# Second cross attention of a two-layer model: the delta scaled in the loop, both norms behind it in parts, and the mixtures fetched in order of use

## The reference, cut to what matters

```python
# fifth: second cross attention, 16 heads of 16, keys and values from audio tokens
delta = ctx @ Wo.T + bo
delta = clip(residual_scale, 0, 0.3) * delta
delta = (delta - mean(delta)) / sqrt(var(delta) + 1e-5) * ln_gamma + ln_beta
x = layernorm(x + delta)
# sixth: experts of the second layer
scores = softmax(x @ gate_weight.T)                 # 64 columns, the 6 largest are kept
flat = w_dense[:, inv_mapping]                      # 8 experts x 8 mixtures
soft = softmax(where(flat == 0, -1e9, flat)); scalar = flat.sum(-1)
# for each of the 8 experts f, with w = soft[f]:
xe = x + w @ muW.T
gate = silu(fused(xe, gW, qa, qb, scale, w)); up = fused(xe, ...)
out += scalar[f] * fused(gate * up, dW, dqa, dqb, ds, w)
y = out + shared(x)                                 # shared: silu(x @ G) * (x @ U) @ D
x = layernorm(x + y)
```

## Time and profile before

| what | value |
|---|---|
| median of three runs | 1113.26 us (1110.69 to 1115.44) |
| the profiled execution | 1109.19 us, its span 1107.4 us |
| mean granted TensorE clock | 0.931 |
| PE busy | 972.9 us, 88% of the span |
| DVE busy | 550.2 us, 50% |
| ACT busy | 362.3 us, 33% |
| POOL busy | 200.1 us, 18% |
| SP's DMA queue, share of 16 engines | 18.2% |

### The profile page before, as it was taken

The page is one execution under the profiler, slowest core; times in us unless marked ns, Lnnn a source line. Parts: engine busy times, 40 slices in busy tenths (PEclk is TensorE's granted clock), DMA queues, the critical chain, the costliest instruction groups (busy, mean ns, idle before and its releaser), DMA issues.

```text
span 1107.4 us, 18950 instructions
## 1 busy us (share of the span) xinstructions
PE 972.9 (88%) x7488; PEld 608.9 (55%) x7488; DVE 550.2 (50%) x1110; ACT 362.3 (33%) x724; POOL 200.1 (18%) x241
## 2 busy tenths in 40 slices
PE   7998879998899999983963899898498999999996
PEld 4664523333468899981452467758364444444443
DVE  2599788885431111015578576536762333233324
ACT  3444346666222233321366354143231000000002
POOL 5021000000012222210026841041000111111110
PEclk9999869999799999995987799998898999999998
DMA  6000000000745455523000202030015022221101
GB/s 235 2 2 1 1 1 2 2 2 1 276 141 180 149 186 188 170 86 115 1 1 1 76 2 97 1 136 3 1 47 119 13 87 87 81 77 66 37 1 38
DMA packets 27242, 75.15 MB, mean 68 GB/s; under 512 B 9860, under 2 KB 17292, under 8 KB 21780
## 3 DMA queue, kind: packets, MB, share of 16 engines
q1 hardware_dynamic: 24948, 67.91, 18.2%
q0 software_dynamic: 2208, 6.03, 1.8%
HBM read 67.48 MB, written 6.46 MB: 67 GB/s over the span
## 4 chain that ended last, share of the span: by engine, by line
PE 70%; DVE 21%; issue 3%; DMA 3%; ACT 3%; SPq 0%; POOL 0%; DVEq 0%; ACTq 0%; POOLq 0%
PE psum L1521 8%; PE psum L1096 8%; PE psum L1108 7%; DVE arena L2082 4%; PE psum L819 3%; PE psum L1525 3%; PE psum L1287 3%; PE psum L1551 3%; PE psum L1509 2%; PE psum L1555 2%; PE psum L1000 2%; DVE arena L2001 2%; DVE arena L2000 2%; PE psum L1546 2%; PE psum L1257 2%
## 5 line engine op out<-in xcount | busy, mean ns | idle before, releaser
L1944 ACT ACTIVATE arena<-psum 128x512 f32<-128x512 f32 (+1 forms) x32 | 19.0, 593 | 227.6 <-PE psum L1525 227.6
L1521 PE MATMUL psum<-arena 128*128 128x512 f32 (+1 forms) x192 | 90.6, 608 | 0.5 <-DVE arena L2530 0.5
L1762 ACT ACTIVATE arena<-psum,arena 128x128 f32<-128x128 f32 x184 | 52.4, 368 | 115.4 <-PE psum L1096 99.1
L2082 DVE TENSOR_REDUCE arena<-psum 128x2 f32<-128x512 f32 x128 | 82.6, 688 | 15.2 <-PE psum L946 13.1
L1096 PE MATMUL psum<-arena 128*128 128x128 f32 x736 | 86.7, 276 | 0.0
L1096 PEld LDWEIGHTS psum<-arena 128*128 128x128 f32 x736 | 84.0, 192 | 2.7 <-issue 2.7
L745 POOL TENSOR_TENSOR arena<-arena 128x512 f32<-128x512 f32 (+1 forms) x32 | 40.4, 1264 | 241.9 <-ACT arena L1944 241.9
L1108 PE MATMUL psum<-arena 128*128 x368 | 83.1, 379 | 0.0
L2229 DVE COPY arena<-psum 128x256 f32<-128x256 f32 x23 | 9.8, 425 | 135.6 <-PE psum L1081 85.2
L1739 ACT ACTIVATE arena<-psum 128x1024 f32<-128x1024 f32 x64 | 65.4, 1024 | 35.4 <-PE psum L968 32.5
L1108 PEld LDWEIGHTS psum<-arena 128*128 128x128 f32 x368 | 68.2, 190 | 8.4
(11 more groups left out here) (371 smaller groups left out, 1818.9 us busy)
## 6 DMA issues: line engine op xcount, KB each, us to landing
arena<-in_w SPq DMA_DIRECT2D x31, 1024.0 KB, 12.5
arena<-in_experts SPq DMA_DIRECT2D x8, 1248.0 KB, 5.9
arena<-mixed SPq DMA_DIRECT2D x16, 256.0 KB
arena<-mixed SPq DMA_DIRECT2D x8, 512.0 KB
arena<-in_ctx SPq DMA_DIRECT2D x2, 1024.0 KB, 7.4
arena<-returned SPq DMA_DIRECT2D x8, 256.0 KB, 5.0
arena<-in_w_xattn SPq DMA_DIRECT2D x1, 1538.5 KB, 9.9
arena<-in_w_ffn SPq DMA_DIRECT2D x1, 1152.0 KB, 5.2
```

What stands on the lines that cost most here:

```text
L1521: pe.matmul(out, e[w][:, k, :], xe6[:, half, k, :], start=(k == 0), stop=False)
L1762: last = act.activation(hidt[:, r % 2, ic * P:(ic + 1) * P], bank(n)[:, i * P:(i + 1) * P], ACT.Gelu, bias=b1_tile[:, r % 4, ic:ic + 1])
L2082: ax_max.by(dve.tensor_reduce(nmx[:, b % 2, :, h], bank(u % 2).rearrange("p (t s) -> p t s", t=2), AX.X, ALU.max, negate=True))
```

## The change

- `delta_stats` gets a fourth instruction, (delta - mean) * gamma, so the step of L2435 is done in the loop, tile by tile.
- Both norms are split. The norm of delta has two parts, tiles 0 to 4 (`FIRST5` = 5) and 5 to 7. The norm of x + delta has two parts, tiles 0 to 3 and 4 to 7. There are four additions of epsilon, four square roots on ACT (the first behind the last exponential of the attention loop, with its table load) and four inversions where there were two of each. The steps of the tiles alternate with `delta_stats(6)` and `delta_stats(7)`, and all go through `do`.
- `turn_x`, `copy_xt` and the logits are done by halves: four tiles transposed, their logits, four tiles transposed, their logits.
- `fetch_mix` issues `wm6` first, then `we6`, then `scale6`, each kind with a semaphore of its own (old semaphores are used again), and PE, DVE and POOL each wait for what they read only.
- PE's order at the start of the expert loop becomes `fuse_in(0)`, `shared_down(1, (0, 1))`, `ranks(0)`, `shared_down(1, (2, 3))`. `fuse_in(0)` waits for the fifth of the six shared products of DVE, since it writes the banks that these free.

The diff, without the new arguments `tiles`, `lo` and `hi` of `turn_x`, `copy_xt` and `ln_sqrt`, and without the waits of PE, DVE and POOL on the split semaphores (`near_in`, `mix_in`, `scale_in`):

```diff
@@ -476,7 +477,8 @@
         sh_h = again("sh_h", onx_ready, B)
         mixed_out = signal("mixed_out")
         mix_in = [signal(f"mix_in_{i}") for i in range(3)]
-        MIX_DMAS = 5
+        near_in = [Signal(loaded[n].sem, 32) for n in ("ident", "w_attn0", "w_xattn0")]
+        scale_in = [Signal(loaded[n].sem, base) for n, base in (("consts", 32), ("consts_late", 32), ("w_route0", 16))]
         scaled6 = signal("scaled6")
         tail_blank = signal("tail_blank")
         mid_dve = again("mid_dve", v_sb, 4)
@@ -593,14 +595,14 @@
             sp.dma_start(w_f1, a["w_ffn1"]).then_inc(loaded["w_ffn1"].sem, 16)
             def fetch_mix(f):
 
-                done, mixed = mix_in[f % BUFS], a["mixed"]
-                w = wide(mixed[f * KX:(f + 1) * KX, :], 1, RX)
+                mixed, buf = a["mixed"], f % BUFS
+                few = mixed[f * KX:(f + 1) * KX, :]
+                for k in range(KC):
+                    sp.dma_start(wm6[32 * k:32 * k + KX, buf, :], few).then_inc(near_in[buf].sem, 16)
                 for half in range(2):
-                    sp.dma_start(we6[64 * half:64 * half + 64, f % BUFS, :], w).then_inc(done.sem, 16)
-                sp.dma_start(scale6[:, f % BUFS, :], mixed[FX * KX + f:FX * KX + f + 1, :].to_broadcast([P, B * S]))\
-                  .then_inc(done.sem, 16)
-                for k in range(KC):
-                    sp.dma_start(wm6[32 * k:32 * k + KX, f % BUFS, :], mixed[f * KX:(f + 1) * KX, :]).then_inc(done.sem, 16)
+                    sp.dma_start(we6[64 * half:64 * half + 64, buf, :], wide(few, 1, RX)).then_inc(mix_in[buf].sem, 16)
+                sp.dma_start(scale6[:, buf, :], mixed[FX * KX + f:FX * KX + f + 1, :].to_broadcast([P, B * S]))\
+                  .then_inc(scale_in[buf].sem, 16)
 
             for f in range(FX):
                 if f == 2:
@@ -1555,13 +1557,14 @@
                     out6_ps.by(pe.matmul(tile_sum(4 * half + t), ha6[:, half, t * P:(t + 1) * P], e["dwx"], start=False,
                                          stop=(n >= STEPS - 2), skip_group_check=True))
 
-            turn_x(4)
             pe.wait_ge(loaded["w_ffn1"].sem, 16)
-            for j in range(NT):
-                pe.wait_ge(xt_sb.sem, 4 * NT + j + 1)
-                for k in range(KC):
-                    last = pe.matmul(bank(4)[:, j * E1:(j + 1) * E1], xt[:, k, j * P:(j + 1) * P],
-                                     f1["gate"][:, k, :], start=(k == 0), stop=(k == KC - 1))
+            for half in (range(0, 4), range(4, NT)):
+                turn_x(4, half)
+                for j in half:
+                    pe.wait_ge(xt_sb.sem, 4 * NT + j + 1)
+                    for k in range(KC):
+                        last = pe.matmul(bank(4)[:, j * E1:(j + 1) * E1], xt[:, k, j * P:(j + 1) * P],
+                                         f1["gate"][:, k, :], start=(k == 0), stop=(k == KC - 1))
             lg6_ps.by(last)
 
             def shared_down(n, tiles):
@@ -1597,13 +1600,15 @@
             for c4 in range(1, len(SHARED)):
                 gate_up(f1["shg"], f1["shu"], c4, 1)
             pe.wait_ge(wt6_sb.sem, wt6_sb.base + 2)
+            pe.wait_ge(sh_h.sem, sh_h.base + 2 * len(SHARED) - 1)
+            fuse_in(0)
             shared_down(1, (0, 1))
+            ranks(0)
+            shared_down(1, (2, 3))
             pe.wait_ge(tail_blank.sem, 1)
-            for step in range(-1, STEPS + 1):
+            for step in range(STEPS + 1):
                 if step + 1 < STEPS:
                     fuse_in(step + 1)
-                if step == -1:
-                    shared_down(1, (2, 3))
                 if 0 <= step < STEPS:
                     features(step)
                 if step + 1 < STEPS:
@@ -1902,13 +1907,16 @@
                 pt5_ready.by(act.activation(pt5[:, b % 2, :].rearrange("p (g n) -> p g n", g=2),
                                             s5[:, b // 2 % 2, :, b % 2 * D:(b % 2 + 1) * D], ACT.Exp,
                                             scale=attend5[:, b:b + 1], bias=off5[:, b:b + 1]))
+                if b == B - 1:
+                    ln_sqrt(4, 0, FIRST5)
                 if b % 2 == 1 and b >= 3:
                     copy_out5(b // 2 - 1)
             copy_out5(NT - 1)
-            ln_sqrt(4)
-            ln_sqrt(5)
-
-            copy_xt(4)
+            ln_sqrt(5, FIRST5, NT)
+            ln_sqrt(6, 0, 4)
+            copy_xt(4, range(0, 4))
+            ln_sqrt(7, 4, NT)
+            copy_xt(4, range(4, NT))
             act.wait_ge(p6_sub.sem, p6_sub.base + 1)
             p6_exp.by(act.activation(prob6, prob6, ACT.Exp))
 
@@ -2412,6 +2420,24 @@
                                             scalar=scale5[:, 0:1], in1=bo5, op0=ALU.mult, op1=ALU.add), y5_read)
                 do(dve.bn_stats(stats[:, j, :], delta5[:, j, :]))
                 do(dve.bn_aggr(mean_var[:, j, :], stats[:, j, :]))
+                do(dve.scalar_tensor_tensor(out=delta5[:, j, :], in0=delta5[:, j, :], scalar=mean_var[:, j, 0:1],
+                                            in1=x1["gamma"], op0=ALU.subtract, op1=ALU.mult))
+
+            def add_eps5(lo, hi):
+                do(dve.tensor_scalar(rstd[:, lo:hi], mean_var[:, lo:hi, 1], EPS, None, ALU.add), ln_var)
+
+            def over_std5(use, lo, hi):
+                dve.wait_ge(ln_std.sem, use + 1)
+                do(dve.reciprocal(rstd[:, lo:hi], std[:, lo:hi]))
+
+            def add_delta(j):
+                do(dve.scalar_tensor_tensor(out=x[:, j, :], in0=delta5[:, j, :], scalar=rstd[:, j:j + 1],
+                                            in1=x[:, j, :], op0=ALU.mult, op1=ALU.add))
+                tile_stats(j)
+
+            def normalise5(j):
+                x_norm.by(dve.tensor_scalar(x[:, j, :], x[:, j, :], mean_var[:, j, 0:1], rstd[:, j:j + 1],
+                                            ALU.subtract, ALU.mult))
 
             LIMIT5 = 50.0 * float(DH1) ** 0.5
             for j in range(NT):
@@ -2425,22 +2451,31 @@
                     divide5(j - 1)
                 if j >= 3:
                     delta_stats(j - 3)
+            add_eps5(0, FIRST5)
             divide5(NT - 1)
-            for j in range(NT - 3, NT):
-                delta_stats(j)
-            do(dve.tensor_scalar(rstd, mean_var[:, :, 1], EPS, None, ALU.add), ln_var)
-            dve.wait_ge(ln_std.sem, 5)
-            do(dve.reciprocal(rstd, std))
+            delta_stats(NT - 3)
             dve.wait_ge(x_beta.sem, NT)
-            each_tile(lambda j: dve.scalar_tensor_tensor(
-                          out=delta5[:, j, :], in0=delta5[:, j, :], scalar=mean_var[:, j, 0:1], in1=x1["gamma"],
-                          op0=ALU.subtract, op1=ALU.mult),
-                      lambda j: dve.scalar_tensor_tensor(
-                          out=x[:, j, :], in0=delta5[:, j, :], scalar=rstd[:, j:j + 1], in1=x[:, j, :],
-                          op0=ALU.mult, op1=ALU.add),
-                      lambda j: dve.bn_stats(stats[:, j, :], x[:, j, :]),
-                      lambda j: dve.bn_aggr(mean_var[:, j, :], stats[:, j, :]))
-            normalise(5)
+            over_std5(4, 0, FIRST5)
+            add_delta(0)
+            add_delta(1)
+            delta_stats(NT - 2)
+            add_delta(2)
+            add_delta(3)
+            delta_stats(NT - 1)
+            add_eps5(FIRST5, NT)
+            add_eps5(0, 4)
+            add_delta(4)
+            over_std5(5, FIRST5, NT)
+            over_std5(6, 0, 4)
+            for j in range(4):
+                normalise5(j)
+                if j >= 1:
+                    add_delta(4 + j)
+            add_eps5(4, NT)
+            over_std5(7, 4, NT)
+            for j in range(4, NT):
+                normalise5(j)
+            dve.wait_ge(x_norm.sem, x_norm.n)
 
             def shared_hidden(m):
                 n, c4 = divmod(m, len(SHARED))
```

More of the change, by code:

```diff
@@ L416, in build @@
         attend5, off5 = arena.take(B), arena.take(B)
+        FIRST5 = 5
         on5, ot5 = arena.take(2, D), arena.take(2, KC, P)
@@ L740, in _ @@
                 if half == 0:
-                    pool.wait_ge(mix_in[f % BUFS].sem, 16 * MIX_DMAS * (f // BUFS + 1))
+                    pool.wait_ge(scale_in[f % BUFS].sem, scale_in[f % BUFS].base + 16 * (f // BUFS + 1))
                 cols = slice(half * BANK, (half + 1) * BANK)
@@ L751, in _, with turn_x @@
             ident = c["ident"]
-            def turn_x(use):
-                for j in range(NT):
+            def turn_x(use, tiles=range(NT)):
+                for j in tiles:
                     t = use * NT + j
@@ L1495, in fuse_in @@
                     pe.wait_ge(experts_in[f % BUFS].sem, 16 * (f // BUFS + 1))
-                    pe.wait_ge(mix_in[f % BUFS].sem, 16 * MIX_DMAS * (f // BUFS + 1))
+                    pe.wait_ge(near_in[f % BUFS].sem, near_in[f % BUFS].base + 32 * (f // BUFS + 1))
                 cols = slice(half * BANK, (half + 1) * BANK)
@@ L1617, in do, with copy_xt @@
                 act.wait_ge(s.sem, s.by(instruction))
```

(14 more changed lines are left out.)

## The result

| | before | change |
|---|---|---|
| median | 1113.26 us | 1102.28 us (1096.34 to 1105.51, five runs) |
| ratio to before | | 0.990, interval 0.9867 to 0.9933 |
| profiled execution | 1109.19 us, span 1107.4 | 1100.47 us, span 1098.6 |

What follows compares the result with a forecast made beforehand. PE was taken to bound the kernel, with 70% of the chain of waits. Gains of 1.4 us (norms) and 7.8 us (mixtures) sum to 9.2, taking 1113.26 to about 1104.0 us; range 1100.5 to 1109.5.

Steps and rivals of the forecast that it cites:

- the sum: Whole kernel: 1.4 us from the norms and 7.8 us from the mixtures, 9.2 us less in all.
- The mixtures' term: Start of the expert loop: small copies issued first land 2.0 us after issue, so `features(0)` starts 7.8 us earlier.
- the cover of the added step: Attention loop: the extra 0.52 us DVE instruction per tile fits DVE's 0.69 us idle per period, cost 0.
- DVE isn't faster: Norms behind the attention loop: DVE ends at about 805.99 instead of 805.4; only PE's work under DVE's gains.
- the norms' term: Norms to logits: transposes and half the logits run under DVE's work, gain 0.7 to 2.1 us, taken as 1.4.
- the same 4.9 us lead to 807.7, before the last logits: Norms: PE, busy without a break from 802.8, gets the full clock back 4.9 us later, at 807.7.
- the second rival: Logits and `gate_up`: clock stays low longer because PE's work comes in pieces, gain only 5.4 us, 1107.9; chance 0.09.
- the prediction's own sign: End of the logits: forecast near 810.2; an end after 811.6 would prove the norms' part wrong.
- The rule I argued against: Transposes before the logits: skill says they don't count for the clock; prediction objected that it rose at 808 after them.

Runs made afterwards that it cites:

- the norms alone: The kernel before with only the norms' part of the change, the mixtures as before: median 1109.88 us, ratio 0.9983 (0.9960 to 1.0007).
- the change again: The change measured once more without any edit, against the kernel before: median 1105.17 us, ratio 0.9927 (0.9904 to 0.9949).

## Why the prediction was right, and where it wasn't

**Right: the sum, the mixtures.** 9.2 us were predicted; 11.0 and 7.3 were measured in two sets of runs, so a forecast this close is also luck. The mixtures' term was 7.8: r fell by 7.6 us in the trace of the change and by 8.1 in the seven later traces of kernels with the whole of this part. Only a detail was mis-sized. In the first trace the second small copy landed 3.19 us after its issue, not 2.0, and `fuse_in(0)` waited 0.44 us. In the seven others `fuse_in(0)` starts without a wait 2.8 us after that issue, so the copy had landed by then. The rule of the Trainium skill ("DMA: Bandwidth & Descriptors", Queues, rings and completion order) is that a queue's descriptors are taken in ring order, and this trace agrees with it: issued first, the copies came 3.2 us after their issue instead of 8.3. The rule speaks of the order of taking, not of landing. That what is issued first also lands first, as the prediction put it, is what this trace shows: the small copies had landed at 840.60, and `scale6`, issued at 839.08, landed at least 8.7 us after its issue.

**Right: the cover of the added step.** `values5` starts at 768.70, 772.80 and 776.90 us in the change, 4.10 apart as before.

**Right: DVE isn't faster.** The norm of tiles 4 to 7 starts 801.29 - 783.22 = 18.07 us after the start of A in the change, where the sum gave 804.63 - 786.38 = 18.25, and they end 0.5 us later than in before.

```profile
801.08 0.18 DVE L2431 RECIPROCAL arena<-arena 128x4 f32<-128x4 f32 x1 [0.34 <-ACT arena L1633]
801.29 1.38 DVE L2439 TENSOR_SCALAR arena<-arena 128x256 f32<-128x256 f32 x4
```

**Wrong: the norms' term, 1.4 us,** by the step "the same 4.9 us lead to 807.7, before the last logits". The trace of before had the clock back 4.9 us after PE's first transpose. That was taken for what always happens, and it had happened once: in all nine other traces without added products it took 14 to 17 us. Trace against trace A is therefore 0.5 us longer, and g 1.2; this is the second rival (chance 0.09). What it said of the change was true, but not its reason, that PE's work comes in pieces: kernels with whole norms and whole logits have the clock low as long. It erred in another thing too: before pays for the low clock as well in most executions, as the medians say, and more, since 6.9 us of its logits lie behind the norms. Against those executions the norms' part gives 2.6 in A and 0.4 to 1.0 in g. The median of the norms alone, 1.9 us lower, lies near the forecast 1.4 (its interval includes no gain), so the number held while its working did not. By the prediction's own sign, logits that end after 811.6, 25.2 us behind the start of A, the norms' part failed: in the change they end at 808.90, 25.7 us behind it. The shape of the gain was right all the same: DVE ends 0.5 us later, and half of the logits lies under its work. Against the usual executions of before this half is worth 3.5 us and not 1.8, since it would have run at the low clock too.

**The rule I argued against.** The Trainium skill ("TensorE: Matmul & The Clock Gate", Part 4: PE-mode transpose) says transposes don't count for the clock as other products do. I let one row speak against it. The later traces agree with it as far as it goes: the clock stayed low through eight transposed tiles. But it also stayed low through all logits, 6.9 us that are products and no transposes, and came back 2 to 5 us after the first product of `gate_up`; of that the rule says nothing. The trace of before remains an exception that the rule doesn't explain. Why its clock came back earlier is open.

**Not foreseen: what the parts are for.** With the step in the loop, splitting brought nothing measurable. With the clock kept full it costs 0.7 us in A. DVE's steps tile by tile are longer, which makes the norms end 3.2 us later (19.45 against 16.28 us behind the start of A in these two traces as well), and half of the logits ahead wins back less of it at the full clock (1.9 us for 16 instructions) than at the low one (3.5 us).

## What to carry to other kernels

Look in more than one trace for the granted clock behind every idle stretch before costing PE's work there; a single execution can show it at its best. While another engine runs a long serial stretch, products that nobody reads keep PE's clock full, and here that took 4.8 us off A and g, about half of what the change gives. Issue first the transfer that is needed first, with a semaphore of its own, and only then put its user at the head of an engine's queue: the second without the first cost 2.5 us in r.

## What the runs showed of the hardware

- The clock stayed low for 14 to 17 us after PE began again with transposes and products of 64 columns, though PE was busy for most of that time; it came back 2 to 5 us after products of 512 columns began. In one trace of the ten without added products it was back after 4.9 us.
- It fell 1.9 to 4.2 us after the end of PE's last product in seven traces (4.2 in that of before, 2.6 in that of the change). In the three others it fell 0.2 to 0.6 us after the start of the last `out5`, which PE had waited 3.24 us for.
- An fp32 product of 128x128 by 64 columns takes nearly twice as long at the low clock as at the full: 3.5 us against 1.9 for 16 instructions.
- Two executions of the same instructions ahead of this stretch can differ by several us (783.2 to 790.1 us). The granted clock differs there: from 100 to 200 us it was 0.86 in the trace of the change and 0.81 in that of the change again, from 600 to 700 us 0.90 and 0.86. Whether that is all of the difference isn't shown.
- Two small DMAs of 32 KB, with nothing ahead of them, from a tensor written just before, landed 3.2 us after the issue of the second in one trace and within 2.8 us in seven others.
